# Self-attention stages: second turn and next scores ahead of the weighing

## The reference

```
scores = q . k / 4      (plus a causal mask, or plus -slope * |i - j|)
probs  = softmax(scores, over the keys)
out    = (probs . v) . Wo + bias
```

## Time and profile before

| | |
|---|---|
| median of three runs | 3068.95 us |
| profiled execution: span | 3070.0 us |
| busy: TensorE, VectorE, ScalarE, GpSimd | 89%, 53%, 47%, 46% of the span |
| mean granted TensorE clock | 0.942 of full speed |
| instructions | 70943 |

### The profile page before, as it was taken

How to read it: one execution, slowest core, us unless ns; L and a number is a source line. 1 busy time by engine, 2 the same in 40 slices (tenths; PEclk the granted TensorE clock), 3 DMA queues, 4 the chain that set the end, 5 groups by cost and what they waited for, 6 DMA issues and landing times.

```text
span 3070.0 us, 70943 instructions
## 1 busy us (share of the span) xinstructions
PE 2724.3 (89%) x25041; PEld 2119.4 (69%) x25041; DVE 1635.4 (53%) x3572; ACT 1435.2 (47%) x4582; POOL 1409.9 (46%) x1645
## 2 busy tenths in 40 slices
PE   7888988569899979969986889999996996999999
PEld 6777776446666656746655767787774665768888
DVE  7999999654356645551126753333333224556643
ACT  4666665444366657733327852222321335773310
POOL 3777777723466755543335652332322223663320
PEclk9999998779999999969997989999995998999999
DMA  3000000100000000141111020000016111010100
GB/s 99 3 2 2 2 2 2 55 30 1 23 15 17 14 20 1 55 146 43 45 64 47 0 94 11 7 10 10 7 54 220 33 32 52 1 48 29 53 10 20
DMA packets 75141, 106.09 MB, mean 35 GB/s; under 512 B 11024, under 2 KB 54672, under 8 KB 74656
## 3 DMA queue, kind: packets, MB, share of 16 engines
q1 hardware_dynamic: 68960, 86.68, 8.5%
q0 software_dynamic: 5952, 16.26, 1.7%
HBM read 88.50 MB, written 14.42 MB: 34 GB/s over the span
## 4 chain that ended last, share of the span: by engine, by line
PE 55%; POOL 4%; DVE 4%; ACT 3%; issue 3%; SPq 1%; DMA 1%; DVEq 0%; ACTq 0%; POOLq 0%
PE up_ps L2490 5%; PE e_out_ps L2508 5%; PE t_ps L664 4%; PE s_ps L650 3%; PE bank_a L1554 3%; PE bank_b L1554 3%; POOL probs L569 2%; PE up_ps L2484 2%; PE bank_a L612 2%; ACT probs L798 2%; PE bank_d L701 2%; PE frame_ps L1633 2%; PE bank_d L620 2%; PE bank_b L1570 2%; PE bank_a L1570 2%
## 5 line engine op out<-in xcount | busy, mean ns | idle before, releaser
L569 POOL TENSOR_TENSOR probs<-probs,inv 128x512 f32<-128x512 f32 x320 | 328.0, 1039 | 274.1 <-DVE inv L919 273.9
L3454 POOL TENSOR_TENSOR hc<-h,bc 128x1024 f32<-128x1024 f32 x128 | 302.0, 2360 | 112.5 <-DVE h L3735 86.4
L798 ACT ACTIVATE probs<-s_ps,negmax 128x128 f32<-128x128 f32 (+1 forms) x768 | 297.7, 415 | 6.4 <-DVE negmax L879 5.0
L3735 DVE TENSOR_TENSOR_SCAN h<-da,dbu_ps 128x1024 f32<-128x1024 f32 x128 | 292.5, 2286 | 11.1 <-DVE dbu_ps L3747 4.4
L664 PE MATMUL t_ps<-ident,probs 128*128 128x128 f32 x1280 | 208.2, 286 | 57.8 <-POOL probs L569 49.2
L664 PEld LDWEIGHTS t_ps<-ident,probs 128*128 128x128 f32 x1280 | 139.2, 141 | 124.7 <-POOL probs L569 59.4
L3682 ACT ACTIVATE da<-dta_ps 128x1016 f32<-128x1016 f32 x128 | 130.3, 1018 | 150.2 <-PE dta_ps L3544 149.9
L3544 PE MATMUL dta_ps<-dt,a_spread 32*128 32x128 f32 x2048 | 155.2, 291 | 43.1 <-ACT da L3682 23.0
L2414 POOL DMA_INDIRECT expert_rows_out<-y,row_to x62 | 61.1, 986 | 268.7 <-DVE y L2773 138.3
L879 DVE TENSOR_REDUCE negmax<-s_ps 128x4 f32<-128x1024 f32 (+1 forms) x128 | 156.6, 1223 | 44.7 <-PE s_ps L650 42.7
L3544 PEld LDWEIGHTS dta_ps<-dt,a_spread 32*128 32x128 f32 x2048 | 130.4, 194 | 67.2 <-ACT da L3682 30.0
(11 more groups left out here) (509 smaller groups left out, 6752.4 us busy)
## 6 DMA issues: line engine op xcount, KB each, us to landing
cT<-in_ctx_turned SPq DMA_DIRECT2D x32, 256.0 KB, 2.6
w_down<-in_L_ffn_w SPq DMA_DIRECT2D x8, 1024.0 KB, 12.3
w_up<-in_L_ffn_w SPq DMA_DIRECT2D x8, 1024.0 KB, 13.5
c_in<-in_ctx SPq DMA_DIRECT2D x16, 256.0 KB, 2.8
w_gate<-in_L_ffn_w SPq DMA_DIRECT2D x8, 512.0 KB, 6.8
w_up<-in_L_ffn_w SPq DMA_DIRECT2D x8, 512.0 KB, 9.0
w_down<-in_L_ffn_w SPq DMA_DIRECT2D x8, 512.0 KB, 9.0
w_gate<-expert_rows_out SPq DMA_DIRECT2D x8, 512.0 KB, 6.6
```

Of the source, the lines that this page charges most:

```text
L569: pool.tensor_tensor(probs[:, u % 2, i], probs[:, u % 2, i], inv[:, u % 2, HB * i:HB * (i + 1)].unsqueeze(2).broadcast_to([P, HB, W]), ALU ...
L798: last = act.activation(probs[:, u % 2, i, k, :], src, ACT.Exp, bias=negmax[:, u % 2, at], accum_out=sums[:, u % 2, at])
L3454: pool.tensor_tensor(hc[:, s % 4], h[:, s % 2], bc[:, j, 1, :].unsqueeze(1).broadcast_to([P, 2 * G, P]), ALU.mult).then_inc(hc_ready.sem, 1)
L3735: dve.tensor_tensor_scan(flat(h[:, s % 2]), flat(da[:, s % 4]), dbu_ps[s % 2][:, :, :, :].rearrange("p i g t -> p (i g t)"), 0.0, ALU.mult ...
```

## The change

On TensorE, `weigh` moves from between the two turns of a step to the place behind the scores. In the context stage `out` and `turn` move ahead of the second turn; in the distance stage `out` does. In the causal stages `out` and `turn` stay last, behind `weigh`. On VectorE `take_context` moves from the start of a step to the place behind `row_max`. `take_k`, `take_v` and the other engines keep their order.

```
--- before.py
+++ after.py
@@ -714,19 +714,22 @@
                         project_qk(b + 1, 1 - j)
                     if u == 1 and left:
                         project_v(b + 1, 1 - j)
-                    if u > 1 or not first:
-                        weigh(*weighing)
+                    ends_one = u == OUT and begun_out(b, first)
+                    if ends_one and (alibi or kt == 2):
+                        out(b - BEHIND, j if BEHIND == 2 else 1 - j, *out_after(b, left))
+                    if kt == 2 and u == NP - 1 and left == 2:
+                        turn(b + 2, j)
                     if u > 0 or not first:
                         turn_probs(turned[0], turned[2], 1)
-                    if alibi and u == OUT and begun_out(b, first):
-                        out(b - BEHIND, j if BEHIND == 2 else 1 - j, *out_after(b, left))
                     if u < NP - 1:
                         score(b, j, u + 1)
                     elif left:
                         score(b + 1, 1 - j, 0)
-                    if not alibi and u == OUT and begun_out(b, first):
-                        out(b - BEHIND, j if BEHIND == 2 else 1 - j, *out_after(b, left))
-                    if u == NP - 1 and left == 2:
+                    if u > 1 or not first:
+                        weigh(*weighing)
+                    if ends_one and not alibi and kt == 1:
+                        out(b - BEHIND, j, *out_after(b, left))
+                    if kt == 1 and u == NP - 1 and left == 2:
                         turn(b + 2, j)
                 if not left:
                     turn_probs(b, NP - 1, 0)
@@ -943,8 +946,6 @@
                         take_k(b + 1, 1 - j)
                     if u == 1 and left:
                         take_v(b + 1, 1 - j)
-                    if u < 2 and not first:
-                        take_context(b - 1, 1 - j, u)
                     invert(b, u, 0)
                     if u > 0 or not first:
                         copy_probs(*((b, u - 1) if u else (b - 1, NP - 1)))
@@ -956,6 +957,8 @@
                         row_max(b, u + 1)
                     elif left:
                         row_max(b + 1, 0)
+                    if u < 2 and not first:
+                        take_context(b - 1, 1 - j, u)
                     if ends_one:
                         (moments if alibi else finish)(b - BEHIND, j if BEHIND == 2 else 1 - j)
                     if u == 0 and left == 2:
```

## The result

The changed kernel takes 3204.67 us (median of four runs, 3195.53 to 3214.28) against 3070.81 us before in the same setting: a ratio of 1.0425, 95% interval 1.0408 to 1.0443, so 130 us slower (the two medians alone differ by 134; the text goes by the ratios). The forecast was 3190, the range 3118 to 3222. The profiled run took 3208.68 us, its span is 3206.0.

A forecast was written before the change was run, and what follows sets the result against it. The prediction took nearly full TensorE and its loop through reciprocal and scaling to bound the kernel. Late turns of 78 us plus 43 us of slower clock made 121 us, so 3190 us, range 3118 to 3222.

The forecast's parts named there:

- The wait that the change turns round: Step 1, VectorE: take_v stands first but waits for a weighing now last on TensorE, delaying reciprocal, scaling and next turn.
- The links from weighing to next turn: Step 1: weighing to take_v 0.78, take_v 0.42, reciprocal to scaling 0.23, scaling to turn 1.10; together 2.53 us.
- One sign: All four stages: VectorE's v copy waits for the weighing about 1.5 us or more each instead of 1.0.
- The sum of the late turns: Four stages, 14 items: 2.0 context, 1.45 last causal, 0.9 first causal, 1.2 distance; 78 us, between 55 and 92.
- the late step: Step 1's next first turn: 1.61 us late in context, 1.68 in last causal taken as 1.45, 0.9 in first causal.
- Step 0: Context and causal stages: no gain counted; context item 2.3 us late if this step is late too.
- step 2 of the context stage: Out now stands between the turns and waits for take_context behind the row maxima: next first turn 0.43 us later.
- The clock: All four stages: longer TensorE waits drop the clock to half; 32 more falls at 1.35 us each, 43 us.
- two falls in three: Share of the 56 items whose wait drops the clock: 37 falls, less the 5 already there.
- (a): Rival: the turns are late but the clock holds, 3147 us; chance 0.28.
- (b): Rival: faster through earlier second turn, scores and reciprocals, 3035 us, or 3061 from the context stage alone; chance 0.05.
- (c): Rival: no change, the late scalings are taken up by TensorE's idle time, 3069 us; chance 0.03.

The follow-up runs named there:

- e1: Kernel after with take_v on VectorE moved from the head of step 1 to behind row_max: 3100.19 us, ratio 1.0073.
- e2: Kernel after with the weighing of step 1 alone put back between the two turns on TensorE: 3078.20 us, ratio 1.0006.
- e8: Kernel before with only step 1's weighing moved behind the scores and step 1's take_context behind row_max: 3196.25 us, ratio 1.0391.
- e5: Kernel after with 6 matmuls on constants added at the end of step 1 on TensorE: 3123.89 us, ratio 1.0165.
- e6: e2 with the distance stage's out also put back, between second turn and scores: 3065.11 us, ratio 0.9969.
- e7: Kernel before with the new order in the two causal stages alone and take_v behind row_max there: 3064.69 us, ratio 0.9971.
- e3: Kernel after with 12 matmuls of 128 columns on constants added at the end of step 1 on TensorE: 3179.42 us, ratio 1.0335.

## Why the prediction was right

**The wait that the change turns round: right.** e1 and e2 each undo only that wait, from either side, and give back five sixths and nearly all of the loss; e8 makes only that wait, with the one copy that has to move, and gets nine tenths of it. The links from weighing to next turn were predicted at 2.53 us and are 2.46 (1018.12 to 1020.58) and 2.54 (2784.51 to 2787.05). One sign failed: the copy of v was to wait 1.5 us or more in all four stages, and in the distance stage it waits 0.3 to 0.4. The forecast's own sum for that stage had said so (0.48 us late), so the sign did not fit the sum.

**The sum of the late turns: right in kind, too large.** 78 us were forecast; e5 has 51. By stage, in items past the stage's start and without a fall (e5 against before; in the distance stage the kernel after, 11.7 to 11.9 us, against 10.7): context 1.1 instead of 2.0, first causal 0.6 instead of 0.9, last causal 1.0 instead of 1.45, distance 1.1 as against 1.2; 14 times their sum is 53. From first turn to first turn (timelines; rows not shown) the late step was forecast well: step 1 is 1.43 late in the context stage (forecast 1.61), 1.5 in the last causal one (1.45) and 0.75 in the first (0.9). What failed is two terms. Step 0, where the weighing and the copy of its result now stand behind the path, had been put at nothing and comes sooner: 0.4 in the context stage, 0.5 in the last causal and 0.15 in the first. And step 2 of the context stage was to be 0.43 late and was not (4.0 us to the next first turn, where it was 4.04): the row maxima began 0.73 us after the reciprocal (1019.25 to 1019.98) and not 1.02, so `out` began 0.85 after the first turn and not 1.2, and second turn to weighing takes 1.6 (1016.48 to 1018.12 in step 1) and not 1.73, since I had counted to the end of the last score matmul. Together these are some 1.5 us an item, or 21 of the 25 us. In the distance stage both parts came out: e8, which leaves `out` in its place, has 11.06 us without a fall, 0.3 more than before, and e6 puts `out` at 0.9.

**The clock: right in kind, too small, and larger than the lateness.** 43 us were forecast; by the ratios of the kernel after and e5 it is 80. The price of a microsecond at half clock was right. The 13 context items of the kernel after spend 85 us at half clock (a mean granted clock of 0.84 over 265 us) and take 35 us longer than e5's, 0.41 us for each; the two causal stages give 0.46, and the forecast's 1.43 us for 3.4 is 0.42. The Trainium skill (TensorE: Matmul & The Clock Gate, Terms) puts the penalty at the throttled time times the share of pulses withheld, by which a microsecond at half clock costs an estimated 0.5. The measured prices lie a little below that. The count of falls was nearly right too: 9, 8, 4 and 7 in the 13 items of the four stages, 28 of 52 against "two falls in three". What failed is the size of a fall, each taken as one in the distance stage (3.4 us at half clock, 1.35 us of time). In the causal and distance stages they were of that length; in the context stage the clock stayed down for 9.5 us on average, and items with a fall took up to 23.05 us, where those without one take 17.6 to 17.7 in e5. At the end of that stage it stayed down from about 1145 to 1168 us, as the windows show, where the kernel before had no fall. The items counted hold 104 of the 136 us by which the two spans differ; of the other 32, 15 lie between the last turn of an input in the context stage and the first of the next stage (45.8 us before, 60.6 after; 52.2 in e5, so that 8 of them are the clock's).

**The two errors nearly cancelled** (27 us too much, 37 too little), so the time is closer than its terms. That is luck.

**Rivals.** (a), the clock holding, is what e5 makes true with its fill: 3124, where (a) had 3147. In the changed kernel the clock did not hold. (b), faster, was decided where the prediction put it: with take_v out of the way (e1, e7) the causal stages gain 0.2 to 0.3 us an item, and the context stage nothing. (c): no slack took up the lateness. The Trainium skill (Perfetto Trace Analysis, Identifying the Most-Contended Engine) judges TensorE's headroom by its weight loads, and at 67% that would have left room. It did not help here: operands came late, and their lateness showed in the time (51 us in e5).

## What to carry to other kernels

Before moving work on one engine, look for every wait on its semaphore on the others, and ask what stands behind each of these waits in its queue: here an edit to TensorE's order hurt through a copy on VectorE that was not edited. Where TensorE is nearly full, such a wait can cost more through the clock than by its length: here 80 us against 51, about half of it in the context stage and at its end, while in the last causal and the distance stage the clock cost less than the lateness. A fill on constants shows how much of a loss is which. An order that loses as a whole may win in the stages where its one bad wait can be moved: e7 keeps the edit in two of the four stages, with the copy of v moved, and is faster than either kernel.

## What was not expected of the hardware

The clock can stay down while TensorE is busy for most of the time: in the context stage after, TensorE was busy for 8.4 of 10 us between 1150 and 1160, at half clock throughout. In the causal and distance stages of the same run falls lasted 3.4 us each, in the context stage 9.5 us on average. Why they last longer there was not tried. A 32-bit matmul of 128 columns on constants took 0.24 us (2.84 us for 12 in e3, two records each); the four transposes of a bank, of the same size and one record each, take 0.66.
